# A new order of TensorE's work in the attention step: whole weightings behind every fourth pair, near scores together, maxima earlier

## The reference

```python
def _strided_allowed(S):
    i = jnp.arange(S)[:, None]
    j = jnp.arange(S)[None, :]
    return (j % STRIDE == 0) | (jnp.abs(i - j) <= LOCAL)      # 4 and 8
...
scores = jnp.einsum('bhqd,bhkd->bhqk', q, k) / jnp.sqrt(jnp.asarray(D, x.dtype))
scores = jnp.where(allowed, scores, -jnp.inf)
attn = jax.nn.softmax(scores, axis=-1)
out = jnp.einsum('bhqk,bhkd->bhqd', attn, v)
...
x = x + _L0_attn_ref(xn, ...) + _L0_ffn_ref(xn, ...)      # ffn: one product with fp8-rounded input
```

## Time and profile before

| | |
|---|---|
| median of 3 runs | 1197.07 us (1196.61 to 1198.26) |
| the profiled execution | 1197.61 us, span 1195.8 us |
| TensorE busy | 1114.0 us, 93% of the span |
| VectorE busy | 996.0 us, 83% |
| ScalarE busy | 803.0 us, 67% |
| POOL busy | 240.8 us, 20% |
| DMA | 124.44 MB, mean 104 GB/s |
| granted clock of TensorE | 0.984 of 2.4 GHz in the mean; about half in the ninth of 40 slices (239 to 269 us), where the attention starts |

### The profile page before, as it was taken

One profiled execution on the slowest core, in us unless ns is written; L12 is line 12 of the kernel. 1 busy time (PEld: TensorE's weight loads), 2 busy tenths in 40 slices (PEclk: granted clock), 3 DMA queues, 4 the chain that ended last, 5 costly groups with the idle time before them and its releaser, 6 DMA issues.

```text
span 1195.8 us, 27662 instructions
## 1 busy us (share of the span) xinstructions
PE 1114.0 (93%) x10178; PEld 562.5 (47%) x10178; DVE 996.0 (83%) x1842; ACT 803.0 (67%) x1528; POOL 240.8 (20%) x318
## 2 busy tenths in 40 slices
PE   5799999999999999999999999999999999999999
PEld 3466666634444444444444444444444444444387
DVE  6778887498999999998999999999999989999333
ACT  3343344327888888888888888888888788888800
POOL 2233333301121212212121212122121212122100
PEclk9899999959999999999999999999999999999999
DMA  4566667632222323223232223222322222232278
GB/s 156 163 189 185 193 201 196 204 95 53 67 69 71 82 64 81 62 78 74 71 75 68 69 72 78 72 76 62 76 76 71 75 68 70 74 78 57 60 255 273
DMA packets 184913, 124.44 MB, mean 104 GB/s; under 512 B 50824, under 2 KB 169352, under 8 KB 184776
## 3 DMA queue, kind: packets, MB, share of 16 engines
q1 hardware_dynamic: 169888, 114.81, 34.7%
q10 hardware_dynamic: 14896, 7.93, 2.5%
HBM read 70.61 MB, written 50.99 MB: 102 GB/s over the span
## 4 chain that ended last, share of the span: by engine, by line
PE 73%; DVE 16%; issue 5%; POOL 3%; ACT 2%; ACTq 0%; DMA 0%; DVEq 0%; POOLq 0%
PE ps_attend L1125 21%; PE ps_attend L1095 11%; PE ps_attend L1065 8%; DVE peak_far L1019 8%; PE ps_attend L1132 5%; PE ps_attend L1069 5%; PE ps_attend L1224 4%; DVE peak_near L1022 3%; PE ps_attend L1071 3%; PE ps_attend L1109 3%; PE ps_project L563 3%; PE ps_project L573 3%; PE ps_attend L1103 3%; POOL y L288 1%; PE ps_project L588 1%
## 5 line engine op out<-in xcount | busy, mean ns | idle before, releaser
L1019 DVE TENSOR_REDUCE peak_far<-ps_attend 128x1 f32<-128x512 f32 x1024 | 652.9, 679 | 44.3 <-PE ps_attend L1095 39.5
L948 ACT ACTIVATE probs<-ps_attend 128x512 f32<-128x512 f32 x1024 | 554.6, 601 | 119.3 <-PE ps_attend L1065 58.2
L1095 PE MATMUL ps_attend<-k_op,q_op 48*128 48x512 f16 x1024 | 326.2, 389 | 49.2 <-DVE peak_far L1019 45.6
L1065 PE MATMUL ps_attend<-q_op,k_op 50*128 50x512 f16 x1024 | 308.6, 382 | 0.8 <-ACT probs L953 0.4
L1125 PE MATMUL ps_attend<-probs,v_op 128*32 128x512 f32 x2048 | 274.5, 608 | 2.8 <-ACT probs L948 2.1
L1022 DVE TENSOR_REDUCE peak_near<-ps_attend 128x4 f32<-128x432 f32 x256 | 154.0, 602 | 34.1 <-PE ps_attend L1109 34.1
L807 POOL TENSOR_SCALAR peak_rest<-peak 128x16 f32<-128x16 f32 x64 | 16.1, 252 | 704.7 <-DVE peak L1003 704.7
L1095 PEld LDWEIGHTS ps_attend<-k_op,q_op 48*128 48x128 f16 x1024 | 84.8, 94 | 140.5 <-DVE peak_far L1019 97.3
L953 ACT ACTIVATE probs<-ps_attend 108x512 f32<-108x512 f32 x256 | 144.8, 597 | 3.5 <-PE ps_attend L1071 3.3
L1065 PEld LDWEIGHTS ps_attend<-q_op,k_op 50*128 50x128 f16 x1024 | 86.2, 94 | 125.4 <-ACT probs L948 82.8
L1103 PE MATMUL ps_attend<-mask_k,mask_q 48*128 48x216 bf16 x512 | 116.7, 259 | 0.4 <-DVE peak_far L1019 0.4
(11 more groups left out here) (87 smaller groups left out, 1017.2 us busy)
## 6 DMA issues: line engine op xcount, KB each, us to landing
v_dram<-v_sb SPq DMA_DIRECT2D x64, 256.0 KB, 3.0
v_op<-v_dram SPq DMA_DIRECT2D x48, 288.0 KB
q_op<-q_parts_dram SPq DMA_DIRECT2D x384, 32.0 KB, 1.9
k_op<-k_parts_dram SPq DMA_DIRECT2D x96, 96.0 KB, 2.6
base<-in_x SPq DMA_DIRECT2D x16, 512.0 KB, 4.9
q_parts_dram<-qk_parts SPq DMA_DIRECT2D x32, 256.0 KB, 3.0
share_rows<-shares_dram SPq DMA_DIRECT2D x256, 32.0 KB, 2.3
attn_dram<-out_rows SPq DMA_DIRECT2D x256, 32.0 KB, 1.7
```

What stands on the lines that cost most here:

```text
L948: ins = nc.scalar.activation(probs[:, r, h], ps_s[st.bank(kind)], ACT.Exp)
L1019: ins = nc.vector.tensor_reduce(peak_far[:, h, tile:tile + 1], bank, AX_X, ALU.max)
L1065: ins = nc.tensor.matmul(bank, k[rows, keys(h, r * P, P)], q[rows, h % PAIR], start=True, stop=True)
L1095: ins = nc.tensor.matmul(bank, q[rows, h % PAIR, tile * P:(tile + 1) * P], k[rows, keys(h, 0, NS)], start=True, stop=True)
```

## The change

The order of a step is rewritten. Each of the five weightings stands behind four pairs: near and far round 3 of the step before, then far rounds 0, 1 and 2. The four near scores follow each other. The units of tile 3 come first, `AHEAD` is 4, so that `maximum()` stands behind the fourth unit, and the transpose `maxima()` stands behind the tenth pair, ahead of a weighting. `turn_sums()` moves from in front of unit 17 to unit 14, between near units (1,1) and (0,0). The weighting that comes last of its step is now far round 3, so `start` and `stop` flags and waits go by a table, `WEIGHINGS`. On POOL the chain of the maxima goes ahead of the multiplication by the shares. `weigh` can be cut in parts, but `SPLIT` is 1. No instruction is added or removed in a step.

```diff
-AHEAD = 10
-TURN = 17
+AHEAD = 4
+TURN = 14
...
-    ("far", 1, 1), ("far", 1, 2), ("far", 1, 3), ("near", 0), ("near", 2),
+    ("far", 1, 1), ("far", 1, 2), ("far", 1, 3), ("far", 2, 0), ("far", 2, 1),
+    ("negmax",), ("far", 2, 2), ("far", 2, 3), ("near", 0), ("near", 1),
+    ("near", 2), ("near", 3), ("far", 3, 0), ("far", 3, 1), ("far", 3, 2),
...
+WEIGHINGS = (("far", 0), ("far", 1), ("far", 2), ("near",), ("far", 3))
+SPLIT = 1
...
         def body(st):
-            if st.exists(-3):
-
-                rows = out_rows[:, (st.n - 3) % OUTS]
-                pool.wait_ge(negmax_ready, min(st.at(1), STEPS))
-                pool.wait_ge(shares_loaded, 16 * HG * st.at(-2))
-                nc.gpsimd.tensor_tensor(rows, rows, share_rows[:], ALU.mult).then_inc(attn_ready, 1)
             if st.exists(1):
 
-                if st.exists(-3):
-                    pool.wait_ge(attn_ready, st.at(-2))
                 pool.wait_ge(peak_ready, st.at(2))
...
+            if st.exists(-3):
+
+                rows = out_rows[:, (st.n - 3) % OUTS]
+                pool.wait_ge(negmax_ready, min(st.at(2), STEPS))
+                pool.wait_ge(shares_loaded, 16 * HG * st.at(-2))
+                nc.gpsimd.tensor_tensor(rows, rows, share_rows[:], ALU.mult).then_inc(attn_ready, 1)
...
+    def weighed(st, kind):
+
+        return ROUNDS * st.at(-1) + WEIGHINGS.index(kind) + 1
...
                     if h == 0 and st.n >= 1:
-                        act.wait_ge(pv_done, ROUNDS * st.at(-1) + r + 1)
+                        act.wait_ge(pv_done, weighed(st, ("far", r)))
...
                     if h == 0 and st.n >= 1:
-                        act.wait_ge(pv_done, ROUNDS * st.at())
+                        act.wait_ge(pv_done, weighed(st, ("near",)))
```

More of the change, by code:

```diff
@@ L612 @@
     ("far", 0, 0), ("far", 0, 1), ("far", 0, 2), ("far", 0, 3), ("far", 1, 0),
-    ("far", 1, 1), ("far", 1, 2), ("far", 1, 3), ("near", 0), ("near", 2),
-    ("far", 2, 0), ("far", 2, 1), ("far", 2, 2), ("far", 2, 3), ("negmax",),
-    ("far", 3, 0), ("far", 3, 1), ("far", 3, 2), ("near", 1), ("near", 3),
+    ("far", 1, 1), ("far", 1, 2), ("far", 1, 3), ("far", 2, 0), ("far", 2, 1),
+    ("negmax",), ("far", 2, 2), ("far", 2, 3), ("near", 0), ("near", 1),
+    ("near", 2), ("near", 3), ("far", 3, 0), ("far", 3, 1), ("far", 3, 2),
     ("far", 3, 3),
@@ L1112, in unit, with weigh @@
             ins.then_inc(u_ready, 1)
-        def weigh(st, d, r):
-            v = v_op[st.parity(d)]
-            if r == 0:
+        def weigh(st, d, kind, part):
+            v, n = v_op[st.parity(d)], CH // SPLIT
+            cols = slice(part * n, (part + 1) * n)
+            if kind == WEIGHINGS[0] and part == 0:
                 if st.queries(d) == 0:
@@ L1121, in weigh @@
                     pe.wait_ge(out_copied, st.at(d))
-            if r < ROUNDS - 1:
+            if kind[0] == "far":
+                r = kind[1]
                 pe.wait_ge(s_used, st.entry(("far", r, HG - 1), d))
                 for h in range(HG):
-                    ins = nc.tensor.matmul(ps_o[h * VW:(h + 1) * VW], v[:, r, h * VW:(h + 1) * VW], probs[:, r, h],
-                                           start=(r == 0), stop=False)
+                    ins = nc.tensor.matmul(ps_o[h * VW:(h + 1) * VW, cols], v[:, r, h * VW:(h + 1) * VW],
+                                           probs[:, r, h, cols], start=(kind == WEIGHINGS[0] and part == 0),
+                                           stop=(kind == WEIGHINGS[-1] and part == SPLIT - 1))
             else:
                 pe.wait_ge(s_used, st.entry(("near", HG - 1), d))
-                for t in range(TT):
+                for t in range(part * TT // SPLIT, (part + 1) * TT // SPLIT):
                     tile = NS // P + st.queries(d) * TT + t
@@ L1133, in weigh @@
                                                v[0:WIN, tile, h * VW:(h + 1) * VW],
[L1134 to L1136 removed]
+                                               probs[0:WIN, ROUNDS - 1, h, t * P:(t + 1) * P],
+                                               start=False, stop=False)
+            if part == SPLIT - 1:
+                ins.then_inc(pv_done, 1)
         def body(st):
@@ L1155, in maxima, with weigh_last, weigh_own @@
                     score(st, ("negmax",))
-            def weigh_last(r):
+            def weigh_last(kind, part):
                 if st.exists(-1):
-                    weigh(st, -1, r)
-            def weigh_own(r):
+                    weigh(st, -1, kind, part)
+            def weigh_own(kind, part):
                 if st.exists():
-                    weigh(st, 0, r)
+                    weigh(st, 0, kind, part)
             far(0, 0)
+            far_unit(3, 2)
+            far(0, 1)
+            far_unit(3, 3)
@@ L1166, in body @@
+            weigh_last(("near",), 0)
+            far(0, 2)
+            far_unit(3, 0)
+            far(0, 3)
+            far_unit(3, 1)
+            far(1, 0)
             far_unit(0, 2)
-            far(0, 1)
+            far(1, 1)
             far_unit(0, 3)
-            weigh_last(3)
-            far(0, 2)
+            weigh_last(("far", 3), 0)
+            far(1, 2)
             far_unit(0, 0)
-            far(0, 3)
+            far(1, 3)
             far_unit(0, 1)
-            far(1, 0)
+            far(2, 0)
@@ L1175, in body @@
+            far_unit(1, 2)
+            far(2, 1)
+            far_unit(1, 3)
+            maxima()
+            weigh_own(("far", 0), 0)
+            far(2, 2)
+            far_unit(1, 0)
+            far(2, 3)
+            far_unit(1, 1)
+            near(0)
             near_unit(1, 0)
-            weigh_last(4)
-            far(1, 1)
-            far_unit(1, 2)
-            far(1, 2)
+            near(1)
+            near_unit(1, 1)
+            weigh_own(("far", 1), 0)
+            near(2)
@@ L1200, in body @@
-            far(3, 1)
-            far_unit(3, 2)
-            far(3, 2)
-            far_unit(3, 0)
-            near(1)
-            far_unit(3, 3)
-            weigh_own(2)
             near(3)
             near_unit(0, 1)
+            far(3, 0)
+            far_unit(2, 2)
+            far(3, 1)
+            far_unit(2, 3)
+            weigh_own(("far", 2), 0)
+            far(3, 2)
+            far_unit(2, 0)
             far(3, 3)
-            far_unit(3, 1)
+            far_unit(2, 1)
         def project(j, n):
```

30 lines of the change are left out of this document (4 added, 26 removed).

## The result

The changed kernel takes 1177.18 us in the median of 4 runs (1173.34 to 1177.81), the kernel before 1196.88 (1196.61 to 1198.26), a ratio of 0.9826 with a 95% interval of 0.9804 to 0.9849. The forecast was 1176. The profiled execution has a span of 1175.3 us.

A forecast was written before the change was run, and what follows sets the result against it. VectorE and TensorE, looping over three unit banks, were taken to bound the kernel. Steps -23.8, first units +3.7, step 0 +0.5, end -0.6 and -0.9 sum to -21.1 us: 1176 us, with 1160 to 1191 for 8 in 10.

The forecast's parts named there:

- The loop of the two engines: TensorE and VectorE over three unit banks set the step: 13.27 us instead of 13.66, -23.8 us over 61 steps.
- The one bubble: VectorE's wait at near unit (0,0), behind near(1,1) and the reciprocal: some 0.55 us a step.
- near scores in a row: Rival, chance 0.22: near units wait until the score has left; step 13.5 to 13.66, time 1190 to 1200 us.
- TensorE fills no bubble: Answers the rival, chance 0.15, that near(0,0) starts together with score near(2): step 13.0, 1160 us.
- K is never waited for: Answers the rival, chance 0.09, that units wait for the K load; 3 us late gives 1221 us.
- The reciprocal: Placed in the bubble at near unit (0,0), it fills 0.16 us of it.
- The transpose: Its cost ahead of a weighting: taken as 0.06 us a step, bounded by 0 and 0.32.
- six units: AHEAD of 4 instead of 10 puts six more units ahead of the first score: +3.7 us.
- Step 0: Near scores side by side lose time while TensorE is slower there: +0.5 us, bounds 0 to 3.
- The end: Six fewer units in the last but one step, -0.6 us, and an earlier last near weighting, -0.9 us.
- The moves priced at nothing: Moved maximum and transpose, later output copy, POOL's new order and earlier need for K: no cost.
- 2.2 us of slack a step: ScalarE's claimed room in each step, with which it catches up within its four banks.

The follow-up runs named there:

- spacing: Kernel before with only two weightings (near keys, far round 0) moved one pair later, so each of the five stands behind four pairs: 1169.66 us, ratio 0.9778.
- turn17: Changed kernel with TURN 17 again, the reciprocal back between two far units: 1173.73 us, ratio 0.981.
- pool_back: Changed kernel with POOL's old order, multiplication by the shares ahead of the chain of the maxima: 1174.08 us.
- balanced: Changed kernel with two near pairs mid-group at the maximum and two behind far 1's weighting, outputs' copy one score earlier, TURN 18: 1154.53 us.
- spread: Changed kernel with one near pair, as third, in each of four groups of four pairs: 1153.68 us, ratio 0.9636.
- spread_pool: `spread` with the two small DMAs of the transposed maxima issued by POOL and not ScalarE: 1142.76 us, ratio 0.955 to the kernel before.
- balanced_pool: `balanced` with the two small DMAs of the transposed maxima issued by POOL and not ScalarE: 1146.79 us.
- near_mid: Changed kernel with near pairs in the middle of their two groups, away from the weightings, and TURN 12: 1153.26 us, ratio 0.9636.
- after_pool: Changed kernel with the two small DMAs of the transposed maxima issued by POOL and not ScalarE: 1176.92 us.

## Why the prediction was right

The mechanism held, and so did the sum, with errors of single terms that partly cancel. That the median came within 1.2 us of the forecast is in part luck: half of the changed kernel's runs took 1173 to 1174, by the moment at which the clock returned.

- **The loop of the two engines** (13.27 walked, 13.31 measured). Counted from score near(2) at 607.89, near unit (0,0) is reduced 0.85 later (608.74; walked 0.85), the weighting of far 2 starts 1.83 later (609.72; 1.83) and the near one 4.35 later (612.24; 4.34). The one bubble stands where it was put, 0.59 for 0.55. The two small errors are the maximum (0.31, not 0.21; the prediction read it from the start of the maximum to the next reduction and not from reduction to reduction) and the transpose (about 0.02, not 0.06). `spacing`, walked to 13.18 and 1168 us, came out at 13.25 and 1169.66.
- **What gave the gain** is the place of the weightings, shown by `spacing`; how much of it is the equal number of pairs between them and how much the neighbour, near(2), that one of them lost, isn't shown. What the prediction didn't say, though its rules gave it: the near scores together work against it, since the two groups with near pairs keep TensorE longer than VectorE: 2.69 and 2.83 us from weighting to weighting (604.20, 606.89 and 609.72), for 2.30 of reductions in each.
- **The rivals**: near units start 0.26 and 0.23 behind their scores (608.15 behind 607.89, 608.60 behind 608.37), so they wait for no score to leave, and near scores in a row stand 0.44 to 0.48 apart; and near unit (0,0) doesn't start with its score, so TensorE fills no bubble. K is never waited for.
- **The reciprocal**: it "fills 0.16" of the bubble was right and without worth (`turn17`).
- **The transpose**: taken as 0.06 and bounded by 0.32; both sides of the weighting cost the same. The Trainium skill, page "TensorEngine Tiling (Array Packing)", section Key Properties, says that a change of tiling mode drains TensorE. The trace agrees with the reading that transpose and weighting share one mode: both have 128*32 in their rows, and the weighting starts 0.33 behind the unit with the transpose between them and 0.32 without. No run here changes the mode between the two.
- **The start**: six units were +3.4 for +3.7. Step 0 was the term that was mis-sized: +1.9 for +0.5 in the profiled execution. The prediction put it down to near scores side by side at the slower clock and took the moment of the clock's return as given; it is this moment that moves the whole time by 4 to 5 us between runs of one kernel. In `turn17`, where the clock returned early, the stretch with step 0 is 3.4 us shorter (14.99 between the same two maxima, against 18.39), and the term is 275.76 - 259.81 - 17.45 = -1.5: outside the bounds of 0 to 3, in which the profiled execution lies. What near scores alone cost in step 0 no run shows.
- **The end**: -2.2 for -1.5. From the last weighting of far round 3 to the output part it was 1137.44 - 1134.69 = 2.75 us, with the near weighting between them, and is 1116.89 - 1115.02 = 1.87 now: 0.9 less, as forecast. The stretch ahead of it, from the mark of step 62 on, was 24.59 and is 23.32, 1.3 less for the 0.6 of the six units: the last steps, in which the units run out, got shorter by their own new order too, which the sum had at 0.
- **The moves priced at nothing** cost nothing: POOL's order (`pool_back`) and the earlier need for K (no wait for it).
- **ScalarE** was written off with "2.2 us of slack a step" from its busy time. In the changed kernel that is harmless. It isn't true as said: its DMA issues take 1.9 us a step of its queue (0.61 and 1.29 in `balanced`), are in no busy row, and leave it idle for 1.1. Moving two of the three to POOL gave back 0.14 of the 0.26 that the walk of `spread` missed and 0.20 of the 0.27 that that of `balanced` missed (`spread_pool`, `balanced_pool`). With the maximum at 0.31, `spread` walks to 12.78 and `spread_pool` measures 12.80; what keeps `balanced_pool` at 12.80, 0.07 above its walk, stays open.

## What to carry to other kernels

Where two engines hand work to each other over a few banks, walk one step with the distances read from the trace (matmul to reduction, release to next matmul) and look, between each two long pieces of the one engine, at how much work both have there: the sum over all such groups of the slower one's time is the step, as long as no third engine holds a bank. In this kernel long pieces at equal distances gave the first gain, and light and heavy pairs mixed and not gathered, with no heavy pair right behind a long piece, the second (`near_mid`, `spread`). Count an engine's DMA issues as its work before calling it idle. And look at the length of every step, not only of a typical one: the long steps of `after_pool` cost 2.3 us, as much as 0.04 us in each.

## What the runs showed of the hardware

- TensorE's granted clock fell to 0.50 between 241 and 246 us, while units alone ran, and stood there until some moment between 265 and 280 us that differed between kernels and between runs of one kernel: 1173 or 1177 to 1178 us. So 3 to 5 us between two kernels with the same step say nothing until the granted clock of the start and the length of every step are compared: between `turn17` and the changed kernel they were the clock, between `after_pool` and `turn17` for the most part three long steps.
- Two DMA issues on ScalarE's queue took 1.29 us and left it idle for 0.89; the same two on POOL took 1.17 there. Once in each of the three kernels that issued them on POOL, the second came 2.9 to 3.1 us late.
- A second near score starts 0.44 us behind a first one that followed its predecessor without a wait (605.66 to 606.10 in the changed kernel), and 0.48 to 0.49 behind one that stood behind a weighting (607.89 to 608.37) or had waited for a bank (609.77 to 610.26 in `balanced`).
